# Strassen attention layer on one core: both vector engines' programs written out call by call, first loads paired, last TensorE phase reordered

## The reference

```
q = cond @ Wq.T + bq                       # one query per batch (2 x 512), 16 heads of 32
k = x @ Wk.T + bk ; v = x @ Wv.T + bv      # x: 2 x 2048 x 512, float32
scores = einsum(q / sqrt(32), k)           # one number per token and head
attn = clip(scores, 0, 1)
out = x + (attn[..., None] * v) @ Wo.T + bo
```

## Time and profile before

| | |
|---|---|
| median of 3 runs | 204.22 us (204.20 to 204.33) |
| profiled execution: time / span in the trace | 204.17 us / 202.3 us |
| TensorE busy | 188.1 us, 93% |
| VectorE busy | 169.2 us, 84% |
| ScalarE busy | 114.3 us, 57% |
| mean DMA rate | 139 GB/s |

### The profile page before, as it was taken

The page is one execution under the profiler, slowest core; times in us unless marked ns, Lnnn a source line. Parts: engine busy times, 40 slices in busy tenths (PEclk is TensorE's granted clock), DMA queues, the critical chain, the costliest instruction groups (busy, mean ns, idle before and its releaser), DMA issues.

```text
span 202.3 us, 2289 instructions
## 1 busy us (share of the span) xinstructions
PE 188.1 (93%) x801; PEld 150.2 (74%) x801; DVE 169.2 (84%) x181; ACT 114.3 (57%) x158; POOL 14.6 (7%) x21
## 2 busy tenths in 40 slices
PE   7899999997899589949999999999999999999983
PEld 2588888875688468836888888878888888878862
DVE  0699798989978859978897889797979799779572
ACT  2779834776762568047574758258654583484210
POOL 7000000000000000102200001002100001031000
PEclk9999999999999969999999999999999999999999
DMA  4999900000470000442999400618982006329966
GB/s 145 370 397 412 370 2 0 2 0 5 134 281 0 0 0 0 70 140 22 211 267 374 165 0 8 138 61 128 235 253 116 0 0 98 113 44 239 218 276 260
DMA packets 9226, 28.09 MB, mean 139 GB/s; under 512 B 1280, under 2 KB 1408, under 8 KB 9088
## 3 DMA queue, kind: packets, MB, share of 16 engines
q1 hardware_dynamic: 7488, 21.67, 28.0%
q0 software_dynamic: 1728, 6.29, 18.1%
HBM read 19.57 MB, written 8.39 MB: 138 GB/s over the span
## 4 chain that ended last, share of the span: by engine, by line
PE 45%; DVE 29%; issue 13%; ACT 9%; DMA 2%; SPq 0%; DVEq 0%; ACTq 0%
PE bank_x L400 6%; DVE work L738 6%; DVE form_lo L710 6%; DVE work L729 6%; ACT form_hi L514 6%; PE bank_z L320 4%; PE bank_z L324 4%; PE bank_z L322 4%; PE bank_y L320 3%; PE bank_z L400 3%; PE bank_y L324 3%; PE bank_y L322 3%; PE bank_y L400 3%; DVE work L771 2%; PE score_bank L380 2%
## 5 line engine op out<-in xcount | busy, mean ns | idle before, releaser
L710 DVE TENSOR_TENSOR form_lo<-work,form_hi 128x1024 fp32r<-128x1024 f32 (+1 forms) x36 | 38.5, 1103 | 10.1 <-ACT form_hi L514 8.7
L514 ACT CAST form_hi<-work 128x1024 fp32r<-128x1024 f32 x28 | 28.4, 1050 | 23.9 <-DVE work L771 11.9
L538 ACT ACTIVATE work<-bank_y,cols 128x512 f32<-128x512 f32 x30 | 19.5, 688 | 8.9 <-PE bank_y L324 8.9
L710 DVE TENSOR_TENSOR form_lo<-x_raw,form_hi 128x1024 fp32r<-128x1024 f32 (+1 forms) x17 | 19.1, 1158 | 6.2 <-ACT form_hi L589 5.0
L320 PE MATMUL bank_x<-form_hi,wo_hi 128*128 128x512 f32 x52 | 20.4, 391 | 2.6 <-ACT work L538 2.6
L691 POOL DMA_DIRECT2D work<-x_t x12 | 10.5, 874 | 165.7 <-DVE work L738 161.5
L324 PE MATMUL bank_x<-form_hi,wo_lo 128*128 128x512 f32 x52 | 20.3, 390 | 0.0
L322 PE MATMUL bank_x<-form_lo,wo_hi 128*128 128x512 f32 x52 | 20.2, 389 | 0.0
L320 PE MATMUL bank_y<-form_hi,wv_hi 128*128 128x512 f32 x48 | 18.8, 392 | 0.8 <-ACT work L538 0.8
L514 ACT CAST form_hi<-x_sum 128x1024 fp32r<-128x1024 f32 x9 | 9.5, 1051 | 17.7 <-DVE x_sum L786 11.6
L729 DVE SCALAR_TENSOR_TENSOR work<-relu,work 128x1024 f32<-128x1024 f32 x16 | 19.2, 1220 | 0.0
(11 more groups left out here) (122 smaller groups left out, 388.2 us busy)
## 6 DMA issues: line engine op xcount, KB each, us to landing
x_raw<-x_t SPq DMA_DIRECT2D x16, 512.0 KB, 7.4
out_t<-work SPq DMA_DIRECT2D x14, 512.0 KB, 3.7
work<-x_t POOLq DMA_DIRECT2D x12, 512.0 KB, 5.6
work<-wv_t SPq DMA_DIRECT2D x4, 256.0 KB, 4.9
work<-wq_t SPq DMA_DIRECT2D x4, 256.0 KB, 7.3
work<-wk_t SPq DMA_DIRECT2D x4, 256.0 KB, 7.9
work<-wo_t SPq DMA_DIRECT2D x1, 1024.0 KB, 10.1
out_t<-work SPq DMA_DIRECT2D x4, 256.0 KB, 2.3
```

Source lines behind the costliest of these rows:

```text
L514: nc.scalar.copy(flat(form_hi, kind), raw(kind, phase)).then_inc(hi_ready[kind], 1)
L538: nc.scalar.activation(result_set(phase)[:, q, j * ROWS:(j + 1) * ROWS], of[:, j, :], ACT.Identity, bias=bias[:, tile:tile + 1], scale=sca ...
L710: return nc.vector.tensor_tensor(to, of, hi.bitcast(F32), ALU.subtract)
```

## The change

1. **ScalarE and VectorE are written out call by call** for all phases, in an order of their own for each phase. The counters of weight parts become one semaphore per part, so that the order of making them is free; `home_free` waits only for the parts that lie in the quarter to be overwritten. The second half of `split_a` (batch 1) moves from phase 0 to phase 2, the lo parts of W22 and S4 of Wo are made earlier and later respectively.
2. **First loads.** The first half quarter of x and Wv's block 0 come in one DMA of 512 KB (4 KB per partition, `first_t[0]`), the second half with block 1 in another, blocks 2 and 3 in a third. The small inputs lie in one tensor. Wq and Wk come in two DMAs each instead of four. W11 is cast by VectorE (`first_hi`), beside ScalarE's cast of x. Reloading x for super 1 waits in addition for the four sums of Wv and for W11's lo part, because block 0 lies in x's buffer.
3. **TensorE.** 8 warm-up matmuls on ones instead of 11 on zeros. In phase 0 the second product is S3 with B11 instead of W12 with B21. In phases 1 and 2 the `spread` matmuls move behind a block product each. The last phase is written out: T2 ahead of B21, T3 ahead of T1.

```diff
-WARM_UP = 11
+WARM_UP = 8
...
-            load_wv(0)
-            for k in range(2):
-                at = slice(k * ROWS, (k + 1) * ROWS)
-                sp.dma_start(x_raw[:, Q11, at], x_t[0, Q11, :, at]).then_inc(x_first[k], 16)
-            load_wv(1)
+            for n, of in enumerate((first_t[0], first_t[1], wv_t)):
+                sp.dma_start(first_pairs[n], of).then_inc(first_loaded[n], 16)
             load_x(0, Q21)
...
+                else:
+
+                    for ready in wv_sum_ready:
+                        sp.wait_ge(ready, 1)
+                    sp.wait_ge(wv_lo_ready[W11], 1)
                 reload_x(s, B11, Q11)
...
-            first_product(banks[0], W11, 1, B11, True, False, None)
-            first_product(banks[0], W12, 2, B21, False, True, first_done)
-            first_product(banks[1], S3, 3, B11, True, False, None)
-            first_product(banks[1], W22, 4, B21, False, True, first_done)
+            opening_product(banks[0])
+            first_product(banks[1], S3, B11, True, False)
+            first_product(banks[0], W12, B21, False, True)
+            first_product(banks[1], W22, B21, False, True)
...
-            spread(0, 0)
-
-            for phase in range(1, LAST + 1):
+            product_b11(1)
+            pe.wait_ge(select_ready, 1)
+            spread(0, 0)
+            product_b21(1)
+            spread(0, 1)
+            product_t2(1)
+            scores(1, 0).then_inc(score_done, 1)
+            product_t3(1)
...
+            product_b11(LAST)
+            product_t4(LAST - 1)
+            product_b22(LAST - 1)
+            product_t2(LAST)
+            product_b21(LAST)
+            product_t3(LAST)
+            product_t1(LAST)
             product_t4(LAST)
             product_b22(LAST)
...
                 elif s == 0:
-                    act.wait_ge(wo_lo_ready, 7)
+                    for form in {Q11: (W11, W12), Q12: (W22,), Q21: (S1, S2), Q22: (S3, S4)}[q]:
+                        act.wait_ge(wo_lo_ready[form], 1)
...
+            copy_b11(2)
+            hi(B11, 3)
+            copy_out21(1)
+            hi(T2, 2)
+            relu_scores(1, 0)
+            hi(T3, 2)
...
+            lo(B22, 2)
+            x_t1(3)
+            lo(B21, 3)
+            split_a(1)
+            lo(T1, 3)
+            x_t2(3)
+            add_out22(2)
+            lo(T2, 3)
+            x_t3(3)
+            context(1, Q11)
```

More of the change, by code:

```diff
@@ new lines, in _ @@
+            relu_scores(1, 0)
+            hi(T3, 2)
+            round_scores(1, 1)
+            hi(T4, 2)
+            hi(B22, 2)
+            hi(B21, 3)
+            copy_u2(2)
+            relu_scores(1, 1)
+            hi(T1, 3)
+            copy_u3(2)
+            hi(T2, 3)
+            copy_b11(3)
+            copy_out21(2)
+            hi(T3, 3)
+            hi(T4, 3)
+            hi(B22, 3)
+            hi(B11, 4)
+            round_scores(2, 0)
+            copy_u2(3)
+            hi(T1, 4)
@@ new lines, in _ @@
+            hi(B21, 4)
+            copy_u3(3)
+            relu_scores(2, 0)
+            copy_b11(4)
+            hi(T2, 4)
+            hi(B11, 5)
+            copy_out21(3)
+            hi(T4, 4)
+            hi(T3, 4)
+            round_scores(2, 1)
+            hi(B22, 4)
+            hi(B21, 5)
+            copy_u2(4)
+            relu_scores(2, 1)
+            hi(T1, 5)
+            copy_u3(4)
+            hi(T3, 5)
+            hi(T2, 5)
+            copy_b11(5)
+            copy_out21(4)
@@ new lines, in _ @@
+            hi(T4, 5)
+            hi(B22, 5)
+            hi(B11, 6)
+            round_scores(3, 0)
+            hi(B21, 6)
+            copy_u2(5)
+            hi(T1, 6)
+            relu_scores(3, 0)
+            copy_u3(5)
+            hi(T2, 6)
+            copy_b11(6)
+            copy_out21(5)
+            hi(B11, 7)
+            hi(T4, 6)
+            hi(T3, 6)
+            round_scores(3, 1)
+            hi(B22, 6)
+            hi(B21, 7)
+            copy_u2(6)
+            relu_scores(3, 1)
@@ L687, in _ @@
+            hi(T1, 7)
+            copy_u3(6)
+            copy_b11(7)
+            hi(T2, 7)
+            copy_out21(6)
+            hi(T3, 7)
+            hi(T4, 7)
+            hi(B22, 7)
+            copy_u2(7)
+            copy_u3(7)
         @block.gpsimd
@@ new lines, in _ @@
+            nc.vector.memset(work[0][:, 0, 0:ROWS], 1.0).then_inc(warm_ready, 1)
+            first_hi(W11, 0)
+            wv_part(W11, 0)
+            first_half(0, first_half_hi, first_half_lo)
+            first_half(1, hi_ready[B11], lo_ready[B11])
+            wv_part(W12, 1)
+            wv_part(S3, 2)
+            wv_part(W22, 3)
+            wv_sum(0)
+            first_lo(B21, Q21)
+            split_cond()
+            first_lo(T3, Q12)
+            wv_sum(1)
+            wv_sum(3)
+            first_lo(B22, Q22)
@@ L1022, in constant_columns @@
-def constant_columns():
+            lo(B11, 3)
+            add_out12(1)
+            context_t4(2)
+            split_scores(1, 1)
+            lo(T3, 2)
+            add_out11(2)
+            lo(T4, 2)
+            wo_sum_part(S4, 3)
+            lo(B22, 2)
[8 more added lines that the diff above has]
+            context(1, Q11)
+            lo(T3, 3)
+            x_t4(3)
```

678 lines of the change are left out of this document (374 added, 304 removed).

## The result

| | before | after |
|---|---|---|
| median (range) of 4 runs, us | 204.21 (203.42 to 204.33) | 189.86 (189.18 to 191.16) |
| ratio, 95% interval | | 0.931 (0.926 to 0.937) |
| profiled execution: time / span, us | 204.17 / 202.3 | 189.18 / 187.4 |
| mean DMA rate, GB/s | 139 | 150 |

What follows compares the result with a forecast made beforehand. TensorE was taken to set the end, its waits coming from queue order. Waits 12.8 + opening 0.35 - new short wait 0.3 = 12.85 us; 202.3 - 12.85 = 189.45 span, + 1.87 = 191.3 us; range 189.6 to 195.5.

Steps and rivals of the forecast that it cites:

- The waits: TensorE's eight waits: 12.8 us lost (9.0 idle, 8 x 0.27, 1.6 slow clock) all go, less 0.3 for a new short wait.
- new short wait: Start of phase 2: TensorE asks for B11's lo part with 0.1 us of slack; one wait of 0.3 us counted.
- The rule of 0.27 us: Each TensorE wait costs, beside its idle time, 0.16 us for the drained matmul and 0.11 for the first after it.
- the gains credited to the same places: TensorE's waits removed: score split and T3 in phase 1, `copy_u3` 2.8 us, `copy_out21` 4.6, T4 in the last phase 1.05.
- The opening: Start: landing kept at 5.7 us, first real matmul 0.6 us earlier at 6.3, clock rise at 10.5; 0.35 us gained.
- VectorE's slack: VectorE: x's reload covered by 0.9 us in phase 1; 94% busy with 12 us to spare, harmless pauses at 145 and 164.
- W11's cast: Opening: VectorE's cast of W11 estimated at 0.43 us, hidden beside ScalarE's 0.62 but for at most 0.07.
- No wait moved: Rival: the waits only move, one inversion in each of seven phases giving back 5.6 us, so 197 us; chance 0.12.
- a later clock: Rival: clock rises later in the opening, eight more slow matmuls cost 1.6 us, so 192.9 us; chance 0.09.
- a slowdown: Rival: VectorE, at 94%, falls behind for good, over 13 us lost in seven phases, so 205 to 208 us; chance 0.03.
- VectorE's slip: Rival: VectorE late in the first 50 us, costing 1 to 3 us at phase 2's start, 192.5 to 194.5; chance 0.22.
- The earlier rise: Rival: clock rises before the first product in the opening, 1.6 us less, so 189.7 us; chance 0.05.

Runs made afterwards that it cites:

- e4: Changed kernel with TensorE's last phase in the order of the kernel before; ratio to the kernel before 0.936.
- e6: Changed kernel with TensorE's `spread` and score matmuls of phase 1 where they were before; ratio to the kernel before 0.942.
- e7: Changed kernel with the four contexts of super 1 ahead of x_t1 of phase 3 in VectorE's queue; ratio to the kernel before 0.936.
- e10: Changed kernel with T2's cast ahead of ScalarE's copies and phase-2 copies waiting for all seven Wo lo parts; ratio to the kernel before 0.930.
- e9: Changed kernel with its first six 256 KB pieces read from the old tensors instead of the packed ones; ratio to the kernel before 0.940.
- e1: Changed kernel with each of its three first loads cut into two DMAs of 256 KB, still packed; ratio to the kernel before 0.933.
- e12: Changed kernel with W11 cast by ScalarE behind x's first half instead of by VectorE; ratio to the kernel before 0.927.
- e5: Kernel before with only TensorE's last phase reordered as in the change; ratio to the kernel before 0.996.
- e3: Changed kernel with W22's Wo lo part moved behind B11's lo part and the score split on VectorE; ratio to the kernel before 0.926.
- e8: Changed kernel with 11 warm-up matmuls on ones instead of 8; ratio to the kernel before 0.926.

## Why the prediction was right, and where it was off

The mechanism was right and one size was off. The span was forecast at 189.45 and measured 187.4; that the time around it fell from 1.87 to 1.8 adds nothing. The range held the median by 0.3 us, because its lower end allowed for an early rise of the clock; the larger part of what made the kernel faster than forecast, the early landing, was not in it.

**The waits (12.5 us net in the sum): right.** All eight waits of the earlier trace rows are gone and the clock is 1.00 in the body. From the 25th real matmul to the last one's start it was 184.53 us and is 172.55 (14.18 to 198.71, 11.21 to 183.76): 12.0 us. The expected new short wait at the start of phase 2 came where the walk had its least slack, 0.38 us against the 0.3 counted; with drain and first step it costs 0.48 to 0.6. Another 0.2 are lost at the thin product (two groups of four take 2.05 us instead of 1.82), which closes the account to 0.1 us. The rule of 0.27 us beside the idle time held: 1.05 in e4, 0.78 + 0.27.

**Which edit bears each wait.** e6, e7, e10 and e4 each bring a named wait back, by the copy, cast or sum that the prediction named. By the ratios their prices are 2.2, 1.0, not resolved, and 0.9 us, by the waits in the traces (with 0.27 each) 3.9, 2.0, 1.3 and 1.05; the gains credited to the same places are 2.6 in phase 1, 2.8, 4.6 and 1.05. In phases 2 and 3 the price is below the gain: an order with slack absorbs part of a single inversion that the old one paid in full. In the last phase, where nothing comes behind, the two are alike. In phase 1 trace and times do not agree on which is larger. So the 4.6 and 2.8 are shown as a total, not edit by edit.

**The opening (0.35 in the sum): mis-sized, and more than the whole error.** The 25th real matmul starts at 11.21, where before it started at 14.18: 2.97 us earlier instead of 0.35 (the prediction's own working, 1.4 x 0.227, gives 0.32). The body gave 0.5 us less than its 12.5, and 2.6 less 0.5 are the 2.05 us of span that the forecast was off. The step that failed is the sentence "The two loads needed are the same 512 KB, so I leave the landing at 5.7". They were ready at 4.06, and the first real matmul started at 4.83, not at 6.3. The bytes were the same and their place in DRAM was not: e9 against e1 shows it. The second part of the error is "If the rise stays at 10.5". The step fell at 5.9 in after's profile, within the warm-ups in e6, e10 and e12 (eight took 3.20 to 3.46 us instead of 3.6; the first real ones then step at about 0.34, between the two), and by about 7 us in the other profiles, and e5, whose opening is the kernel before's, ran at the fast step from 7.22. So 10.5 was chance in one profile, and a forecast must not take the moment of the rise from one execution. It also makes the 2.97 look larger than the change is: against e5's 13.04 it is 1.8 us. The Trainium skill (TensorE: Matmul & The Clock Gate, "What's actually happening") says that the number of slow matmuls at the start varies from run to run of one kernel; the profiles here agree, with at least 8 slow real ones in before and none in e5, which has the same opening. How much of the time's spread of 2 us it makes in unprofiled runs stays open.

**VectorE's slack: right in the later phases, not at the reload.** Busy 90%. It paused for ScalarE 1.68 us at 145.73 and 1.43 at 164.09 (forecast 1.9 each), without harm. The reload of x was 0.62 us late for x_t3 (26.22), against 0.9 us of slack forecast: VectorE was there 2.1 us earlier than walked (25.60 against 27.7), the load only 0.6 us. As the walk said of this place, the lateness went on down VectorE's queue; it reached TensorE as the 0.38.

**W11's cast: small, its worth open.** It was priced by ScalarE's 0.62 us beside it, which hides it but for up to 0.07. It takes 0.57 in after and between 0.43 and 0.71 in the other profiles, so the estimate of 0.43 by the Trainium skill (VectorE: DVE Perf Modes, "The perf-mode tier table") is met in two of ten (e7, e9) and otherwise exceeded, in four by more than ScalarE's 0.62 hides. e12, with the two casts one after the other, has 0.3 us more of span and no longer time.

**The rivals.** No wait moved, and neither a later clock nor a slowdown came. VectorE's slip came at the place that its rival named, with 0.38 us instead of 1 to 3, and is what the sum had as its short wait. The earlier rise (0.05, 189.7 us) nearly did, with two to three slow real matmuls left, on top of a landing that no rival held.

## What to carry to other kernels

When two busy engines both have idle time, look at who stands at the head of the queue between them: ScalarE was idle 7.10 us ahead of one cast, and moving instructions, with no work saved, was worth 12 us. Check each move for what it needs to arrive: put into the kernel before by themselves, the paired loads gained nothing, since the second product asked for the block that they push back. Lay the first bytes in DRAM as they are wanted, packed, and take them in few DMAs; count the start-up clock as a range and not as a moment.

## What was not expected of the hardware

- **The layout of the source sets the early DMA rate.** From 2 to 4 us: 172 to 176 GB/s (before, e5), 208 (e9), 315 (e1, packed, 256 KB each), 371 (after, packed, 512 KB each; 338 to 389 in its variants). First data ready at 5.7 to 6.0, 5.37, 4.03 and 4.06 us. In e9 it is the piece cut out of Wv's rows of 8 KB that is late (4.2 us from issue), not the one cut out of x's rows of 4 KB (2.6).
- **The third of three first loads lands with a scatter** of 6.8 to 8.2 us in nine kernels whose loads are the same (6.83 in e12, 8.16 in e4). With a landing at 7.93 (e10) and 8.06 (e6) TensorE waits for it 0.42 and 0.53 us, with one at 7.1 to 7.25 (e3, e7, e8) not at all.
- **Warm-ups on zeros do as well as on ones** (0.9254 and 0.9312, intervals overlapping), and 8 as well as 11 (0.9312 and 0.9257).
